# Expert steps of 256 rows with the first-layer weights as the stationary operand, in a mixture-of-experts layer on one Trainium2 core

## The chip, the core and the metric

The kernel runs on one core of one Trainium2 chip. The metric is the device time of one execution in microseconds (us). A core has five engines with instruction streams of their own: TensorE (PE, with its weight loads shown apart as PEld), VectorE (DVE), ScalarE (ACT), GpSimd (POOL) and SyncE (SP, which here only issues transfers). They meet through semaphores. Sixteen DMA engines move the data.

## What is computed

The reference is one transformer layer: attention, a layer norm, a mixture of experts, and a second layer norm. B is 4, L is 2048, D is 256, so there are 8192 tokens.

```python
x = _layernorm(x + attention(x, ...), axis=-1)   # linear (cosformer) attention, 16 heads
# the second part, tokens = x.reshape(-1, 256)
logits = tokens @ router_w.T                     # 8 experts
topv, topi = jax.lax.top_k(logits, 2)
w = jax.nn.softmax(topv, axis=-1)
gate = zeros((T, 8)).at[arange(T)[:, None], topi].add(w)
for e in range(8):
    h = gelu(tokens @ w1[e].T)                   # w1[e] is 512 x 256, exact gelu
    y = h @ w2[e].T                              # w2[e] is 256 x 512
    out = out + gate[:, e:e + 1] * y
x = _layernorm(x + out, axis=-1)
```

## The kernel before

Every product is made in three passes: each operand is split into a high part (a copy to the fp32r type) and a low part (the rest), and high x high, high x low and low x high are summed in PSUM.

**Stage 1** (up to about 302 us) takes the tokens in 32 pairs of 128-row tiles: keys, values, queries, the running attention state, and for pairs nine places back the attention, the output projection, the layer norm and the routing. Each routed token row is scattered (L1602, an indirect DMA of GpSimd) into `expert_rows` in DRAM, in the region of each of its two experts. ScalarE splits one half of the weights of the last expert, GpSimd the rest.

**Stage 2** runs through 135 steps (STEPS) of 128 rows. A table in `steps` says for each step which rows and which expert it takes. For a step s:

- SP's `gather(s)` (L457) loads 128 rows from `expert_rows` into one of NXG = 8 buffers `xg`. First it waits in `freed(s)` until the rows of step s - 8 have been sent, then it reads the row number from the table.
- TensorE turns them (`rows_transposed`, L714, 2 transposes). ScalarE copies the result as the high part of `xgT` (L961), VectorE makes the low part (L1399).
- TensorE makes the hidden layer (`hidden`, L725): the rows are stationary, the weights move in 6 products of 512 columns. ScalarE makes the gelu (L989) into `hg`.
- TensorE turns the gelu (`hidden_transposed`, L755, 4 transposes), ScalarE and VectorE split it into `hT` (L993, L1471).
- TensorE makes the output (`outputs`, L737): 12 products of 256 columns. VectorE multiplies by the gate and adds the row (`gated`, L1407), in place in `xg`. GpSimd sends the rows to `token_rows` by an indirect DMA (`send`, L1683).

TensorE's order is written by hand: turn the rows of s + 1, hidden layer of s, output of s - 1, turn the gelu of s. Between these stand the pieces of the last pairs (attend L578, attention_transposed L601, project_out L630, rank L642 to L646), at places that `hook(s)` gives: from step 7 on six steps for each of eight pairs. VectorE's order in a step is `rows_low(s + 1)`, `gated(s - 1)`, the low part of `hT`, and then the pair's piece. 73 steps (FULL_STEPS) are sure to be full tiles of the first 20 pairs. For the rest a second table is made: `place` on VectorE (L1292 to L1328), a product that turns it (`table_turned`, L697), and a copy (L1332). SP then writes eight tiles of padding rows behind the regions (L484) before it gathers on.

From step 92 on the second layer norm runs beside the experts, in ticks, four to three steps: SP's `load(c)` (L495) fetches 1 MB of `token_rows` for 512 tokens, VectorE sums, takes statistics and scales (L1424, L1430, L1435, L1440), ScalarE normalises (L973) and issues the store (L980). After the last step the remaining chunks follow. The loads are issued by SP too, between its gathers: three at once after gather 96, and then one every three steps.

```python
def freed(s):
    sp.wait_ge(s_y[s % NXG], s // NXG * 16)
```

Of the kernel before, what the change touches and what calls it, by code (L numbers as in the profile page):

```python
# [23 lines left out]
F32 = mybir.dt.float32  # L24
# [9 lines left out]
P = 128  # L34
# [22 lines left out]
REGION = T + P  # L57
STEPS = TOPK * T // P + E - 1
EARLY_PAIRS = NPAIR - PB - 4
FULL_STEPS = 73  # L60
# [5 lines left out]
LEVEL_STEPS = tuple((TOPK * PAIR * n + E * (P - 1)) // P for n in LEVEL_PAIRS)  # L66
TAIL_STEP = LEVEL_STEPS[0] + 5
TICK_STEPS = 3
# [6 lines left out]
for _name, _n in (("ident", P), ("block", P), ("heads", HH), ("experts", E), ("region", E), ("sin", NT_B),  # L75
                  ("cos", NT_B), ("dst", 2 * TOPK), ("step", 1), ("before", P),
                  ("region_parts", E), ("pair", NPAIR),
                  ("upto", E * E)):
    CO[_name] = (NCONST, NCONST + _n)
    NCONST += _n  # L80


def shape_constants():
# [7 lines left out]
    put("block", p[:, None] // HD == p[None, :] // HD)  # L91
# [11 lines left out]
    put("region_parts", np.where(p[:, None] < P - 1, REGION // P - 1, REGION // P + P - 1) * np.arange(E)[None, :])  # L103
# [5 lines left out]
def build(nc, x, xT, WqT, bq, WkT, bk, WvT, bv, WoT, Wo, bo, bo_columns, rwT, w1T, w2T, consts, out):  # L109
    ctx = ExitStack()  # L110
    first = ExitStack()
    ex = nc.dram_tensor("expert_rows", (E * REGION + P, ROW), F32).ap()
    yd = nc.dram_tensor("token_rows", (TOPK * T, D), F32).ap()
    with ctx:
# [11 lines left out]
        gX, gH, gT, gY = bK, bST, bV, bQ  # L126
# [3 lines left out]
        half_neg = sb("half_neg", [4])  # L130
        e_square = sb("e_square", [2])
        gelu_first = sb("gelu_first", [2])
# [4 lines left out]
        tail = sb("tail", [ROW])  # L137
# [17 lines left out]
        steps = sb("steps", [2 * P], I32)  # L155
# [8 lines left out]
        WE = 2 * KD * F  # L164
        HALF = KD * F
        LATE = 1
        EARLY = E - LATE
        NXG = 8
        XG_SLOTS = (2, 3, 4, 0, 1, 5, 6, 7)
        FFN_WORDS = NXG * ROW + 2 * 2 * KD * P + F + 2 * KF * P + 2 * D  # L170
        raws = ExitStack()
        rwk, rwv, rwq, rwo = (sb(n, [KD, D], F32, raws) for n in ("raw_wk", "raw_wv", "raw_wq", "raw_wo"))
        raws.close()
        whole = ExitStack()
        w = sb("w", [E, 2, WE], F32R, whole)
        whole.close()
        sb("w_early_place", [EARLY - 1, 2, WE], F32, first)
        sb("w_high_place", [WE], F32, first)
        wraw = sb("wraw", [2, HALF], F32, first)
# [6 lines left out]
        sb("xraw_begin", [HALF - 3 * D - E - 2 * KD * E], F32, first)  # L186
# [3 lines left out]
        vs = sb("vs", [2, KD, 2, NQ, VQ], F32, first)  # L190
        wk = sb("wk", [2, KD, KE], F32R, first)
        bvb = sb("bvb", [D], F32, first)
        st32 = sb("st32", [KD, 2, NW], F32, first)
# [21 lines left out]
        vare = sb("vare", [2], F32, first)  # L215
        rstd = sb("rstd", [2], F32, first)
# [7 lines left out]
        shift1 = sb("shift1", [2], F32, first)  # L224
        oh = sb("oh", [2, TOPK, E], F32, first)
        dl = sb("dl", [2], F32, first)
        dls = sb("dls", [2], F32, first)
        el = sb("el", [2], F32, first)
        el1 = sb("el1", [2], F32, first)
        idx = sb("idx", [2, 2, TOPK], U32, first)  # L230
        upto_first = sb("upto_first", [1, E, E], F32, first)
# [3 lines left out]
        late = ExitStack()  # L235
        sb("w_place", [EARLY, 2, WE], F32, late)
        w_late_raw = sb("w_late_raw", [LATE, 2, WE], F32, late)
        late.close()
        sb("w_whole_place", [E, 2, WE], F32)
        xgT = sb("xgT", [2, 2, KD, P], F32R)  # L240
        hg = sb("hg", [F])
        sb("xg_place", [2 * D])
        hT = sb("hT", [2, KF, P], F32R)
        sb("xg_begin", [2 * 2 * KD * (NQ - 1)])
        xg = sb("xg", [NXG, ROW])
# [20 lines left out]
        s_wraw = [sem("s_wraw0"), sem("s_wraw1")]  # L266
# [132 lines left out]
        def _(sp):  # L399
# [59 lines left out]
            def freed(s):  # L459

                sp.wait_ge(s_y[s % NXG], s // NXG * 16)

# [1315 lines left out]
```

## Time and profile before

| what | value |
|---|---|
| time, median of 3 runs | 849.87 us (847.88 to 852.35) |
| span of the profiled execution | 841.6 us |
| TensorE busy | 793.9 us, 94% |
| VectorE busy | 566.7 us, 67% |
| ScalarE busy | 461.0 us, 55% |
| GpSimd busy | 434.3 us, 52% |
| DMA | 106.64 MB, 127 GB/s in the mean |
| mean granted TensorE clock | 0.984 of full speed |

The profile shows one execution. Its span is the time from the first to the last instruction and is 8.3 us under the median of the timed runs, which also holds what lies around it. Matmuls are pipelined: the time of a group of n products is n times the pace plus the latency of the last one. Busy times of engines that are not the bound cost nothing in themselves.

### The profile page before, as it was taken

How to read it: one execution, taken by the hardware profiler on the slowest of the kernel's cores; microseconds unless marked ns; L12 is line 12 of the kernel's file. 1: busy time of each engine (PE TensorE's matmuls, PEld its weight loads, DVE VectorE, ACT ScalarE, POOL GpSimd, SP SyncE). 2: the span in 40 equal slices, each digit the busy share in tenths (PEclk: the TensorE clock that was granted, in tenths of full speed). 3: DMA queues.
4: the chain of work that ended last, by engine and by line, in shares of the span. 5: the costliest groups of instructions: out<-in, count | busy, mean ns of one | idle time of the engine just before them, and what ended most of it. 6: DMA issues, size and time to landing. Idle time of an engine off the chain costs nothing.

```text
span 841.6 us, 22076 instructions
## 1 busy us (share of the span) xinstructions
PE 793.9 (94%) x6684; PEld 732.7 (87%) x6684; DVE 566.7 (67%) x1816; ACT 461.0 (55%) x1044; POOL 434.3 (52%) x545
## 2 busy tenths in 40 slices
PE   4999999999999979999999999999999999999990
PEld 4887899899899969999999999989999999999980
DVE  3435788888888857766676666664444477777773
ACT  4656677667777644454444445434444446556663
POOL 3985477677677755544444454542222234444442
PEclk9999999999999989999999999999999999999995
DMA  6444033333333333323323323233322545666644
GB/s 205 160 150 127 26 102 122 113 110 108 108 103 102 98 131 117 119 90 96 99 93 96 108 88 105 87 100 107 99 78 74 179 133 193 228 226 223 220 175 173
DMA packets 56468, 106.64 MB, mean 127 GB/s; under 512 B 9261, under 2 KB 37551, under 8 KB 54448
## 3 DMA queue, kind: packets, MB, share of 16 engines
q1 hardware_dynamic: 41296, 63.25, 24.5%
q0 software_dynamic: 12624, 33.84, 11.0%
q10 hardware_dynamic: 2448, 8.26, 2.7%
q8 instruction: 58, 0.95, 0.5%
q14 instruction: 42, 0.34, 0.1%
HBM read 61.91 MB, written 44.32 MB: 126 GB/s over the span
## 4 chain that ended last, share of the span: by engine, by line
PE 61%; DMA 1%; DVE 1%; ACT 1%; issue 1%; SPq 0%; POOLq 0%; POOL 0%; ACTq 0%
PE PS L737 23%; PE PS L725 22%; PE PS L755 7%; PE PS L714 4%; PE PS L578 2%; PE PS L630 2%; DMA z<-token_rows 1%; PE PS L601 0%; PE PS L541 0%; DMA token_rows<-xg 0%; DMA expert_rows<-rows,idx 0%; PE PS L632 0%; DMA xg<-expert_rows 0%; ACT rows L862 0%; PE PS L614 0%
## 5 line engine op out<-in xcount | busy, mean ns | idle before, releaser
L1683 POOL DMA_INDIRECT token_rows<-xg x135 | 135.1, 1000 | 271.6 <-DVE xg L1407 251.1
L737 PEld LDWEIGHTS PS<-w,hT 128*128 128x128 f32 x1620 | 211.5, 190 | 12.0 <-issue 1.9
L725 PE MATMUL PS<-w,xgT 128*128 x810 | 222.0, 409 | 0.0
L737 PE MATMUL PS<-w,hT 128*128 x1620 | 217.2, 284 | 0.8 <-ACT hT L993 0.8
L725 PEld LDWEIGHTS PS<-w,xgT 128*128 128x128 f32 x810 | 143.2, 189 | 24.6
L1602 POOL DMA_INDIRECT expert_rows<-rows,idx x128 | 133.9, 1046 | 56.1 <-issue 27.8
L993 ACT ACTIVATE hT<-PS 128x512 fp32r<-128x512 f32 x135 | 80.8, 598 | 135.6 <-PE PS L755 135.6
L989 ACT ACTIVATE hg<-PS 128x512 f32<-128x512 f32 x135 | 80.7, 598 | 120.6 <-PE PS L725 120.3
L1471 DVE TENSOR_TENSOR hT<-PS,hT 128x512 fp32r<-128x512 f32 x135 | 93.4, 692 | 75.9 <-ACT hT L993 75.9
L1399 DVE TENSOR_TENSOR xgT<-PS,xgT 128x256 fp32r<-128x256 f32 x135 | 56.9, 422 | 77.8 <-ACT xgT L961 76.3
L755 PE MATMUL PS<-cst,hg 128*128 128x128 f32 x540 | 81.1, 273 | 0.0
L541 PE MATMUL PS<-wk,xs 128*128 128x264 f32 x384 | 64.3, 304 | 14.5 <-DVE wv L1340 8.4
L1407 DVE SCALAR_TENSOR_TENSOR xg<-PS,xg 128x256 f32<-128x256 f32 x135 | 65.0, 482 | 14.0 <-PE PS L737 4.9
L541 PEld LDWEIGHTS PS<-wk,xs 128*128 128x128 f32 x384 | 51.2, 192 | 21.2 <-ACT vs L853 11.8
L578 PE MATMUL PS<-sts,qs 128*128 128x272 f32 x384 | 60.7, 294 | 2.7 <-DVE sts L1091 2.4
L755 PEld LDWEIGHTS PS<-cst,hg 128*128 128x128 f32 x540 | 62.7, 141 | 0.1
L714 PE MATMUL PS<-cst,xg 128*128 128x128 f32 x270 | 52.3, 276 | 5.0 <-DMA xg<-expert_rows 4.0
L541 PE MATMUL PS<-wv,xs 128*128 128x256 f32 x384 | 56.9, 285 | 0.0
L614 PE MATMUL PS<-xs,wq 128*128 128x256 f32 x384 | 56.8, 294 | 0.0
L630 PE MATMUL PS<-wo,aT 128*128 128x264 f32 x384 | 56.5, 286 | 0.0
L578 PEld LDWEIGHTS PS<-sts,qs 128*128 128x128 f32 x384 | 52.0, 191 | 4.0 <-issue 3.0
L961 ACT ACTIVATE xgT<-PS 128x256 fp32r<-128x256 f32 x135 | 51.2, 379 | 3.4 <-PE PS L714 3.4
(179 smaller groups left out, 1272.8 us busy)
## 6 DMA issues: line engine op xcount, KB each, us to landing
xg<-expert_rows SPq DMA_DIRECT2D x135, 130.0 KB, 2.1
z<-token_rows SPq DMA_DIRECT2D x15, 1024.0 KB, 7.8
xraw<-in_xT SPq DMA_DIRECT2D x32, 256.0 KB
xtok<-in_x SPq DMA_DIRECT2D x32, 256.0 KB, 2.8
out_y<-z ACTq DMA_DIRECT2D x15, 512.0 KB, 3.4
wraw<-in_w1T SPq DMA_DIRECT2D x7, 512.0 KB, 3.9
wraw<-in_w2T SPq DMA_DIRECT2D x7, 512.0 KB, 4.0
token_rows<-xg POOLq DMA_INDIRECT x135, 2.6
```

Source lines behind the costliest of these rows:

```text
L541: return nc.tensor.matmul(PS[:, bank, 0:columns], xs[:, rep % 2, a, k, h * P:(h + 1) * P], weights[:, b, k, :], start=(n == 0), stop=(n == ...
L578: mm = nc.tensor.matmul(PS[:, bN + half, 0:2 * NW], qs[:, a, half, h * P:(h + 1) * P], sts[:, b, half].rearrange("p a b -> p (a b)"), star ...
L630: nc.tensor.matmul(PS[:, bank, 0:KE], aT[:, a, k, h * P:(h + 1) * P], wo[:, b, k, :], start=(n == 0), stop=False)
L714: mm = nc.tensor.transpose(PS[:, gX, k * P:(k + 1) * P], xg[:, XG_SLOTS[s % NXG], k * P:(k + 1) * P], ident)
L725: mm = nc.tensor.matmul(PS[:, gH, :], xgT[:, s % 2, a, k, :], w[:, bass.ds(e, 1), b, k * F:(k + 1) * F].rearrange("p o f -> p (o f)"), sta ...
L737: return nc.tensor.matmul(PS[:, gY, 0:D], hT[:, a, k, :], w[:, bass.ds(e, 1), b, HALF + k * D:HALF + (k + 1) * D] .rearrange("p o f -> p ( ...
L755: mm = nc.tensor.transpose(PS[:, gT, k * P:(k + 1) * P], hg[:, k * P:(k + 1) * P], ident)
L989: nc.scalar.activation(hg[:], PS[:, gH, :], ACT.Gelu, scale=2.0).then_inc(gelu_ready, 1)
L993: nc.scalar.activation(hT[:, 0].rearrange("p k t -> p (k t)"), PS[:, gT, :], ACT.Copy)\
L1471: nc.vector.tensor_tensor(hT[:, 1].rearrange("p k t -> p (k t)"), PS[:, gT, :], hT[:, 0].rearrange("p k t -> p (k t)").bitcast(F32), ALU.s ...
L1602: nc.gpsimd.indirect_dma_start(ex, bass.IndirectOffsetOnAxis(ap=idx[:, slot, h, k:k + 1], axis=0), rows[:, slot, h, k, :], None).then_inc( ...
L1683: nc.gpsimd.indirect_dma_start(yd, bass.IndirectOffsetOnAxis(ap=xg[:, XG_SLOTS[s % NXG], C_DST:C_GATE].bitcast(U32), axis=0), xg[:, XG_SLO ...
```

## The change

A step takes 256 rows (TILE), and there are 71 of them. What it does:

- **Hidden layer.** The weights of the first layer are now stationary and the rows move: 24 products of 256 columns for 256 rows, in place of 12 of 512 columns. The result has the hidden units on the partitions, which is the form that the output product wants, so the 8 transposes of the gelu for 256 rows go, and `hidden_transposed` with them.
- **Weights.** The first-layer weights of all experts lie unsplit in `w1`. A step ahead ScalarE (`first_weights_high`) copies the 128x1024 weights of the step's expert as the high part, and VectorE (`first_weights_low`) makes the low part, in two buffers `w1s`. The second-layer weights are split by GpSimd in stage 1, as before, and lie in `w2`. The late split of the last expert at the end of stage 1 goes.
- **Elementwise work.** The gelu and its split stay in two halves of 128x512 each for 256 rows. The split now reads `hg` from SBUF and not from PSUM.
- **Row buffers.** NXG = 4 buffers of 256 rows in place of 8 of 128. A gather moves 256 rows, two neighbouring rows to a partition. Each step's rows go out in two sends, and `gather(s)` waits for both sends of step s - 4.
- **Orders.** TensorE's order in a step is: hidden s (two parts), turn the rows of s + 1 (4 transposes), output of s - 1 (two parts). The pieces of pairs and ticks keep their places in half steps v = 2s and 2s + 1. VectorE's order is `first_weights_low(s + 1)`, `rows_low(s + 1)`, two `hidden_low`, pair part 2s, two `gated(s - 1)`, pair part 2s + 1.
- **Tables.** FULL_STEPS is 33. The eight padding tiles are now 256 rows each, copied from DRAM to DRAM. The first three loads of the second layer norm follow gather 51.
- The mask `block` goes (the constant `heads` is read in its place), and some small tiles share one allocation.

The core of the diff:

```diff
-STEPS = TOPK * T // P + E - 1
+TILE = 2 * P
+REGION = T + TILE
+STEPS = TOPK * T // TILE + E - 1
-FULL_STEPS = 73
+FULL_STEPS = -(-(TOPK * PAIR * EARLY_PAIRS - E * (TILE - 1)) // TILE)
-TAIL_STEP = LEVEL_STEPS[0] + 5
-TICK_STEPS = 3
+TAIL_HALF = 2 * LEVEL_STEPS[0] + 6
+TICK_HALVES = 3
-        NXG = 8
+        NXG = 4
...
-            def gather(s, place):
+            def gather(s):
-                sp.dma_start(xg[:, XG_SLOTS[s % NXG]], ex[bass.ds(row, P), :]).then_inc(s_xg[s % NXG], 16)
+                sp.dma_start(xg[:, XG_SLOTS[s % NXG]], ex[bass.ds(row, TILE), :].rearrange("(p h) c -> p h c", h=2))\
+                    .then_inc(s_xg[s % NXG], 16)
...
-                sp.wait_ge(s_y[s % NXG], s // NXG * 16)
+                sp.wait_ge(s_y[s % NXG], s // NXG * 32)
...
-                sp.dma_start(ex[bass.ds(row, P), :], tail[:]).then_inc(s_tail, 16)
+                sp.dma_start(ex[bass.ds(row, TILE), :].rearrange("(p h) c -> p (h c)", h=2),
+                             ex[E * REGION:, :].rearrange("(p h) c -> p (h c)", h=2)).then_inc(s_tail, 16)
...
-                if s == LEVEL_STEPS[0] + NXG + 1:
+                if s == LEVEL_STEPS[0] + NXG:
                     sent(LEVEL_STEPS[0])
                     for n in range(LOADS):
                         load(n)
                 for c in range(LOADS, LEVEL_CH[1]):
-                    if s == LEVEL_STEPS[0] + NXG + TICK_STEPS * c:
+                    if s == LEVEL_STEPS[0] + NXG + 3 + (TICK_HALVES * (c - LOADS) + 1) // 2:
...
+            def hidden(s, part):
+                if part == 0:
+                    pe.wait_ge(xglo_ready, s + 1)
+                    pe.wait_ge(w1_low, s + 1)
                 if s >= 1:
+                    pe.wait_ge(gelu_ready, 2 * (s - 1) + part + 1)
+                for f in range(2):
+                    c0 = (2 * part + f) * P
+                    m = 0
+                    for k in range(KD):
+                        for a, b in ((0, 0), (1, 0), (0, 1)):
+                            mm = nc.tensor.matmul(PS[:, gH[part], f * TILE:(f + 1) * TILE],
+                                                  w1s[:, s % 2, b, k * F + c0:k * F + c0 + P],
+                                                  xgT[:, s % 2, a, k, :], start=(m == 0), stop=(m == 3 * KD - 1))
...
+            for s in range(STEPS):
+                hidden(s, 0)
+                ranks(2 * s)
+                hidden(s, 1)
+                if s < STEPS - 1:
+                    rows_transposed(s + 1)
+                after = expert(s + 1) if s < STEPS - 1 else None
+                pair_part(2 * s)
+                if s > 0:
+                    outputs(s - 1, before, 0)
+                ranks(2 * s + 1)
+                if s > 0:
+                    outputs(s - 1, before, 1)
+                pair_part(2 * s + 1)
...
+            def first_weights_high(s):
+                if s >= 2:
+                    act.wait_ge(h_done, 2 * (s - 2) + 2)
+                e = nc.values_load(steps[0:1, s:s + 1], engines=[ENG.Activation], min_val=0, max_val=E - 1)
+                nc.scalar.activation(w1s[:, s % 2, 0], w1[:, bass.ds(e, 1)].rearrange("p o f -> p (o f)"), ACT.Copy)\
+                    .then_inc(w1_high, 1)
...
+            def first_weights_low(s):
+                e = nc.values_load(steps[0:1, s:s + 1], engines=[ENG.DVE], min_val=0, max_val=E - 1)
+                dve.wait_ge(w1_high, s + 1)
+                nc.vector.tensor_tensor(w1s[:, s % 2, 1], w1[:, bass.ds(e, 1)].rearrange("p o f -> p (o f)"),
+                                        w1s[:, s % 2, 0].bitcast(F32), ALU.subtract).then_inc(w1_low, 1)
...
-            for s in range(STEPS):
+            for s in range(2 * STEPS):
-                send(s)
+                if s >= 2:
+                    send((s - 2) // 2, s % 2)
```

## Rows read from the trace of the kernel before

**Rows 1.** The page: busy time, share of the span and instructions of each engine.

```profile
PE 793.9 (94%) x6684; PEld 732.7 (87%) x6684; DVE 566.7 (67%) x1816; ACT 461.0 (55%) x1044; POOL 434.3 (52%) x545
```

**Rows 2.** Stretches: length, busy time of each engine, granted clock, DMA share, GB/s.

```profile
350.00:550.00 200.00, 200.00 (x1462) 185.56 (x1461) 135.67 (x419) 96.08 (x191) 99.93 (x124) 1.00 0.31 98
700.00:800.00 100.00, 100.00 (x683) 91.93 (x682) 74.97 (x213) 60.65 (x125) 42.43 (x49) 1.00 0.65 218
```

**Rows 3.** Timeline, one plain step on TensorE: start, duration, engine, line.

```profile
604.20 0.60 PE L755 MATMUL PS<-cst,hg 128*128 128x128 f32 x4
...
604.64 0.38 PE L714 MATMUL PS<-cst,xg 128*128 128x128 f32 x2
...
604.78 1.64 PE L725 MATMUL PS<-w,xgT 128*128 x6
...
606.25 1.60 PE L737 MATMUL PS<-w,hT 128*128 x12
...
607.69 0.60 PE L755 MATMUL PS<-cst,hg 128*128 128x128 f32 x4
```

**Rows 4.** Timeline of ScalarE: the same piece of two pairs, six steps apart.

```profile
374.65 0.59 ACT L871 ACTIVATE aT<-PS 128x512 fp32r<-128x512 f32 x1
...
399.45 0.59 ACT L871 ACTIVATE aT<-PS 128x512 fp32r<-128x512 f32 x1
```

**Rows 5.** Groups by line: VectorE's elementwise work (busy, mean ns, idle before).

```profile
L1471 DVE TENSOR_TENSOR hT<-PS,hT 128x512 fp32r<-128x512 f32 x135 | 93.4, 692 | 75.9 <-ACT hT L993 75.9
L1407 DVE SCALAR_TENSOR_TENSOR xg<-PS,xg 128x256 f32<-128x256 f32 x135 | 65.0, 482 | 14.0 <-PE PS L737 4.9
L1399 DVE TENSOR_TENSOR xgT<-PS,xgT 128x256 fp32r<-128x256 f32 x135 | 56.9, 422 | 77.8 <-ACT xgT L961 76.3
```

**Rows 6.** Timeline where stage 1 ends: the split of 128x1024 weights.

```profile
300.33 1.07 ACT L955 ACTIVATE w<-w_late_raw 128x1024 fp32r<-128x1024 f32 x1
...
301.57 1.78 DVE L1393 TENSOR_TENSOR w<-w_late_raw,w 128x1024 fp32r<-128x1024 f32 x1
...
302.35 3.63 POOL L1613 TENSOR_TENSOR w<-w_late_raw,w 128x256 fp32r<-128x256 f32 x4
...
305.95 0.66 PE L714 MATMUL PS<-cst,xg 128*128 128x128 f32 x2 [3.97 <-DMA xg<-expert_rows]
```

**Rows 7.** Timelines of VectorE, GpSimd and SP: gated, its send, the gather that follows.

```profile
639.33 0.48 DVE L1407 SCALAR_TENSOR_TENSOR xg<-PS,xg 128x256 f32<-128x256 f32 x1
...
640.63 0.97 POOL L1683 DMA_INDIRECT token_rows<-xg  x1 [2.49 <-DVE xg L1407]
...
643.79 0.34 SPq L457 DMA_DIRECT2D xg<-expert_rows  x1
```

**Rows 8.** Transfers, 360 to 500 us: count, KB each, us from issue to landing.

```profile
xg<-expert_rows SPq DMA_DIRECT2D x34, 130.0 KB, 2.1
token_rows<-xg POOLq DMA_INDIRECT x35, 2.5
```

**Rows 9.** Transfers, 700 to 800 us; columns as in rows 8.

```profile
z<-token_rows SPq DMA_DIRECT2D x10, 1024.0 KB, 7.7
token_rows<-xg POOLq DMA_INDIRECT x29, 5.0
```

**Rows 10.** DMA, 671 to 672.5 us: the first three loads under way, a gather behind.

```profile
DMA packets 86, 0.66 MB, mean 437 GB/s; under 512 B 6, under 2 KB 6, under 8 KB 6
...
xg<-expert_rows SPq DMA_DIRECT2D x1, 130.0 KB, 4.7
```

**Rows 11.** Timeline at the second table: `place` on VectorE, and TensorE's wait.

```profile
558.61 0.41 DVE L1292 TENSOR_TENSOR o<-cst,seg_len 128x256 f32<-128x256 f32 x1
...
562.08 0.15 DVE L1328 TENSOR_SCALAR table<-table 128x1 f32<-128x1 f32 x1
...
562.29 0.38 PE L697 MATMUL PS<-cst,table 128*2 128x128 f32 x2 [1.33 <-DVE table L1328]
```

**Rows 12.** Timeline of SP: the eight padding tiles.

```profile
582.05 8.36 SPq L484 DMA_DIRECT2D expert_rows<-tail  x8
```

More of the change, by code:

```diff
@@ L214, in build @@
         mv = sb("mv", [2, 2], F32, first)
-        vare = sb("vare", [2], F32, first)
-        rstd = sb("rstd", [2], F32, first)
+        pairs = sb("pairs", [8, 2], F32, first)
+        vare, rstd, shift1, dl, dls, el, el1 = (pairs[:, n] for n in range(7))
         rows = sb("rows", [2, 2, TOPK, ROW], F32, first)
@@ L815, in _ @@
                         table_turned(SECOND_MADE, bA)
-            outputs(STEPS - 1, before)
+            before, now = None, expert(0)
+            for s in range(STEPS):
[12 more added lines that the diff above has]
+                pair_part(2 * s + 1)
+                before, now = now, after
+            for h in range(2):
+                outputs(STEPS - 1, before, h)
         @block.scalar
@@ L1019, in _ @@
                         normalise(j, j // 2, True, j % 2)
-                for t in ticks(s):
+                for t in ticks(v):
                     tail_part(t)
+            for s in range(STEPS):
+                if s < STEPS - 1:
+                    first_weights_high(s + 1)
+                for part in range(2):
+                    gelu(s, part)
+                if s < STEPS - 1:
+                    rows_high(s + 1)
+                for part in range(2):
+                    hidden_high(s, part)
+                pair_part(2 * s)
+                pair_part(2 * s + 1)
             for t in TICKS_LEFT:
@@ L1321, in place @@
                 made(base + 12)
[L1322 removed]
+                nc.vector.scalar_tensor_tensor(out=table[:, 1:2], in0=const("step"), scalar=float(TILE), in1=table[:, 1:2],
                                                op0=ALU.mult, op1=ALU.add).then_inc(table_step, 1)
@@ L1331, in steps_from @@
                 dve.wait_ge(tbl_done, which + 1)
-                nc.vector.tensor_copy(steps[0:2, which * P:(which + 1) * P], PS[0:2, bank, P:2 * P])\
+                begin, end = ((0, FULL_STEPS), (FULL_STEPS, P))[which]
+                nc.vector.tensor_copy(steps[0:2, begin:end], PS[0:2, bank, P:P + end - begin])\
                     .then_inc(table_step, 1)
@@ L1566, in _ @@
                     tail_part(t)
-            gated(STEPS - 1)
+            for s in range(STEPS):
+                if s < STEPS - 1:
+                    first_weights_low(s + 1)
+                    rows_low(s + 1)
+                for part in range(2):
+                    hidden_low(s, part)
+                pair_part(2 * s)
+                if s > 0:
+                    for h in range(2):
+                        gated(s - 1, h)
+                pair_part(2 * s + 1)
+            for h in range(2):
+                gated(STEPS - 1, h)
             for t in TICKS_LEFT:
@@ L1696, in tail_part @@
                     deviation(c)
-            for s in range(STEPS):
+            for s in range(2 * STEPS):
                 if s < 2:
@@ L1740, in _ @@
                     tail_part(t)
+            for h in range(2):
+                send(STEPS - 1, h)
             for t in TICKS_LEFT:
```

390 lines of the change are left out of this document (172 added, 218 removed).

## The prediction

> **What bounds the kernel now.** I read the page first: TensorE is busy for 94% of the span, the next engine for 67% [rows 1]. Then the stretches: from 350 to 550 us and from 700 to 800 us TensorE has no idle time and the full clock [rows 2]. So stage 2 takes what TensorE's instructions take, and the timeline of one plain step gives their pace [rows 3]. The step is 607.69 - 604.20 = 3.49 us (3.48 below). A group of n products lasts n - 1 paces and one latency, so the 12 products of 256 columns, which start 1.44 us ahead of the next group, have a pace of 0.120 us. The 6 of 512 columns take 1.47 us, the four transposes of the gelu 0.44 us (0.109 each), the two of the rows 0.14 us up to the start of the hidden layer. In the steps with pairs six steps take 399.45 - 374.65 = 24.80 us [rows 4], so that a pair's pieces take 24.80 - 6 x 3.48 = 3.9 us of TensorE.
>
> **TensorE's work after.** 256 rows need 24 + 24 products of 256 columns and 4 transposes: 48 x 0.120 + 4 x 0.109 = 6.20 us, against 6.96 us for two steps before. No row shows these stationary weights with moving rows, but the shape is that of the output product, so I take its pace. The bounds are 0.107 (256 columns at 2.4 GHz) and 0.123 (half of 1.47 / 6) for the hidden layer's 24: 5.9 to 6.3 us. But there are 71 steps for 135 / 2 = 67.5, because each expert's last tile is padded to 256 rows: 71 x 6.20 = 440.2 against 135 x 3.48 = 469.8. That is **-29.6 us**, and it is all that the change can win. (The Trainium skill, "TensorE: Matmul & The Clock Gate", section "Back-to-back issue gap", speaks against the exchange of 12 products of 512 columns for 24 of 256: in a stream of weight loads and products it has 0.131 us for 512 columns and 0.081 for 128, about 0.098 for 256 in between, an estimate from that page. By it the hidden layer goes from 1.57 to 2.35 us for 256 rows, 55 us more in 71 steps, where the rows have 2.94 and 2.88 us, 4 us less; the forecast would be some 925 us. The trace does not agree: it has 0.245 and 0.120 us, nearly in proportion to the columns, and it decides.)
>
> The pipeline holds a step of rows more at each end, and a step is twice as long. The last output takes 2.9 us for 1.4, and a second send follows it; the first gather, transposes and split are larger by some 1 us. **+4 us.** Stage 1 is bound by TensorE too and loses only work of GpSimd, ScalarE and VectorE that lies beside it: 0.
>
> **VectorE.** An operation of 512 columns takes 0.69 us, of 256 0.42 us [rows 5], so one of 1024 about 1.24 us; the one row with 1024 has 1.78 us, with GpSimd at its own split beside it [rows 6]. I take 1.24, as GpSimd's splits are over. A step costs 1.24 + 0.69 (rows) + 0.69 + 0.61 (gelu) + 0.48 + 0.42 (gated) = 4.1 us. A pair's pieces are 135.7 / 200 x 24.80 = 16.8 less 6 x 1.60, 7.2 us [rows 2, 5]. Three steps then hold 12.4 + 7.2 = 19.6 us in 3 x 6.20 + 3.9 = 22.5: it fits, but not evenly. The step with halves 1 and 2 of a pair has over half of the 7.2 us: 4.1 + 3.9 = 8.0 against 6.20 + 1.2 on TensorE, which waits for the attention's result. I take 0.8 us for each of eight pairs, and 0.2 for sends that GpSimd's scatters hold up: **+8 us** (0 to 16). (A rule of the Trainium skill speaks against these splits: "SBUF — State Buffer", section "Who interferes with whom", says that a VectorE instruction with two SBUF inputs and a GpSimd one that reads SBUF block each other. The 1.78 us agree with it. With 1.78 in each step three steps hold 21.2 us, still under 22.5.) ScalarE has 1.07 us of new copy [rows 6] and at most 5.7 us in a step: cover enough.
>
> **The row buffers.** This is where I expect the gain to go. Rows of step s must be out before gather(s + 4). After the output of s TensorE has hidden, transposes, output, hidden before it needs the rows of s + 4: 3 x 2.88 + 0.44 = 9.1 us. Before it had eight steps less two, over 20 us. The chain now: gated 0.5; the first send starts 640.63 - 639.81 = 0.8 later; the second is 1.3 behind it (0.97 and a gap); landing 2.5 [rows 8]; SP issues 643.79 - 640.63 - 2.5 = 0.7 after that [rows 7]; a gather of 130 KB lands in 2.1 [rows 8]. Twice the rows with twice the run for a descriptor I put at 2.5, between 2.1 and 4.2. Sum: 8.3 us. It fits by 0.8 us where nothing disturbs it.
>
> From the second layer norm on something does. The send's median landing goes from 2.5 to 5.0 us while loads of 1 MB are in flight, 7.7 us each [rows 9]. In the new order a load stands right behind a gather, and both sends that free the next buffer fall into it. 2.5 more less 0.8 to spare, and tick work of VectorE ahead of `gated`, up to 0.9: about 2 us for each of the ten loads c = 3 to 12, **+20 us** (5 to 30). The first three loads stand between gathers 51 and 52. 3.15 MB at 437 GB/s are 7.2 us, and a gather behind them took 4.7 us where 2.1 is usual [rows 10, 8]. With four buffers gather 52 is needed 6.2 us after gather 51 was: **+6 us** (3 to 8).
>
> **The second table.** `place` takes 558.61 to 562.23, 3.6 us, and TensorE waits 1.33 us at its end [rows 11], since the turning product comes a step later. After, both stand in one step, and TensorE comes to it as VectorE begins: +2.3 us. Then the eight padding tiles take SP 8.4 us [rows 12], plus 2 for landing and 0.7, between gathers 32 and 33, where 6.2 + 0.8 are to be had, partly under the first stall: +3.2. **+5.5 us** (2 to 10).
>
> **The clock.** After an idle stretch of 4.0 us TensorE's first transposes took 0.66 for 0.38 us [rows 6, 3], which is the 1.2 GHz level. Three of the new stalls are that long. I take **+2 us** (0 to 8).
>
> **Sum.** -29.6 + 4 + 8 + 20 + 6 + 5.5 + 2 = +15.9 us. The profiled 841.6 us become 857.5; with the 8.3 us by which the median stands above its span, 866.
>
> **The rivals.**
> A. *The buffers never run out*: sends land as fast as before or the loads leave room. Then -29.6 + 4 + 7 + 2.3 = -16: 833 to 834 us, faster. For it: the plain steps fit. Against it: the landing of 5.0 us. It decides if the chain stays under 9.1 us with a load in flight. 0.18.
> B. *The loads cost a quarter*: 0.5 us each, 5 in place of 20: 851 us. It would be so if only one of the two sends meets the load. 0.13.
> C. *The gather of 256 rows takes 3.5 to 4.2 us*. The chain is 9.3 to 10.0 us, over 9.1 in every step, shared over the two steps of the loop: up to 0.45 us in 43 steps outside the pairs, 20 us more: 886 us. For it: twice the bytes. Against it: the fixed part is not doubled. 0.12.
> D. *VectorE becomes the bound in the ticks*, in place of the buffers. The 683 products from 700 to 800 us are 28.5 steps and 38 ticks, so a tick costs it (74.97 - 28.5 x 1.60) / 38 = 0.8 us [rows 2, 5]; 2.7 ticks and 4.1 us are 6.2 us a step, level with TensorE, and 6.8 with the slow split: 0 to 13 us in 21 steps upon A, 840 in the middle. 0.09.
>
> The forecast has 0.48, within 856 to 880 us.
>
> **Range and chances.** About 0.5% is what a measurement of this kernel can tell from no change: 845.6 to 854.1. Faster: A, most of D: 0.25. Same: most of B and a little of the forecast's low end and of D: 0.11. Slower: 0.64. Cases of both signs hold most of the chance, so the range reaches into A: 838 to 886.
>
> **What would show it.** Product starts 0.120 us apart in the hidden layer, and plain steps of 6.2 us, confirm TensorE's part. In the windows from the first tick on TensorE should show idle time ended by the DMA of `xg` (some 25 us in all), at L714's successor, and none in the plain steps between table and ticks; sends should land in about 5 us there. If TensorE has no such waits, A holds; waits in plain steps too speak for C; waits of TensorE for VectorE's `xgT` or `w1s` in the ticks for D. At the second table there should be a wait of over 3 us for `table`, and one for `xg` after it. The prediction is wrong above all if a send and a load in flight share the DMA engines otherwise than in the rows.

## The result, and the profile after

The changed kernel takes 943.64 us (932.11 to 948.42), the one before 849.54 in the same runs: **a ratio of 1.102, 95% interval 1.096 to 1.108**. Two of the four runs of the changed kernel, over 1.5% above its fastest, are left out of the ratio, by which the change costs some 86 us; comparisons below go by such ratios, each against the kernel before as it ran beside that variant, times 846 us, about its time throughout. The forecast of 866 us, and the top of its range, 886, are far too low. The profiled execution took 932.1 us, with a span of 930.3.

The page, its busy times and two of its rows of 40 slices, to be held against [rows 1]:

```profile
PE 801.9 (86%) x7136; PEld 761.2 (82%) x7136; DVE 622.1 (67%) x1836; ACT 529.6 (57%) x1064; POOL 454.9 (49%) x517
...
PE   5999999999998688888889888878999978888880
...
PEclk9999999999999799999999999989999999989995
```

TensorE is busy for 86% of a longer span, and it holds 8 us more of busy time than before where the sum said 30 less. Three stretches, with the columns of [rows 2]: pair steps, plain steps, ticks.

```profile
350.00:550.00 200.00, 172.20 (x1369) 166.08 (x1368) 136.93 (x358) 106.42 (x174) 106.93 (x110) 0.97 0.28 87
640.00:700.00 60.00, 56.29 (x442) 53.95 (x441) 32.61 (x51) 32.41 (x53) 21.91 (x18) 0.97 0.26 80
740.00:850.00 110.00, 92.36 (x685) 88.56 (x684) 76.97 (x187) 63.04 (x106) 43.73 (x42) 0.92 0.50 177
```

There is idle time in each, in the plain steps too, where the forecast had none. What ended TensorE's idle time from 306 us on (engine, line, releaser; total us, times, longest):

```profile
PE PS L698 <- DMA xg<-expert_rows: 57.4, 31, 4.5
PE PS L562 <- DVE qs L1211: 6.8, 6, 1.6
PE PS L726 <- issue: 5.4, 23, 0.4
PE PS L626 <- DVE o L1072: 3.9, 1, 3.9
```

31 times the transposes of the rows (L698, in the kernel before L714) wait for a gather. The longest of these waits, 4.5 us for the very first rows, is no loss of the change: the kernel before has it too, with 3.97 us [rows 6]. The other 30 are new. One plain step, followed from its last output product to the step that takes its buffer (timelines of VectorE, GpSimd, SP and TensorE; steps 37 and 41):

```profile
661.37 3.04 PE L713 MATMUL PS<-xgT,w1s 128*128 128x256 f32 x24
...
661.57 0.88 DVE L1448 SCALAR_TENSOR_TENSOR xg<-PS,xg 128x256 f32<-128x256 f32 x2 [0.94 <-PE PS L726]
...
662.88 1.55 POOL L1710 DMA_INDIRECT token_rows<-xg  x1 [4.20 <-DVE xg L1448]
664.73 0.97 POOL L1710 DMA_INDIRECT token_rows<-xg  x1 [0.30 <-issue]
...
667.85 0.33 SPq L437 DMA_DIRECT2D xg<-expert_rows  x1
...
664.25 0.60 PE L698 MATMUL PS<-cst,xg 128*128 128x128 f32 x4
664.61 3.11 PE L726 MATMUL PS<-w,hT 128*128 x24
...
670.78 0.66 PE L698 MATMUL PS<-cst,xg 128*128 128x128 f32 x4 [0.19 <-DMA xg<-expert_rows]
671.64 3.23 PE L726 MATMUL PS<-w,hT 128*128 x24 [0.20 <-issue]
```

The chain is 670.78 - 661.57 = 9.21 us from the start of `gated`, for the predicted 8.3. To it come the 0.20 us for which TensorE is already at its next hidden layer (661.37) before `gated` starts: 9.41. The room, which counts from there, is 9.1. And behind a wait the output products start 0.86 us after the transposes (671.64 - 670.78), without one 0.36 (664.61 - 664.25).

A wait costs more than itself. After 2.54 us the output group takes 3.91 us for 3.11; the granted clock is 0.65 from 434 to 438 us and 0.93 from 438 to 442:

```profile
434.47 0.66 PE L698 MATMUL PS<-cst,xg 128*128 128x128 f32 x4 [2.54 <-DMA xg<-expert_rows]
...
436.61 3.91 PE L726 MATMUL PS<-w,hT 128*128 x24
```

To see where the time lies I read the starts of the low split of the rows (L1431) off VectorE's timeline in each run's profiled execution, and took differences between steps (us, us a step in brackets). Steps 3 to 30 hold the pairs, 30 to 39 the second table and what follows it, 50 to 52 the first three loads, 52 to 70 the ticks. Each row is a single execution, and two of them can differ by several us in a stage that the edit does not touch: `small_loads` has 81.0 us from step 39 to 50 and the changed kernel 73.6. Differences of that size between rows show nothing by themselves.

```
                            3-30          30-39        39-50        50-52       52-70
changed kernel (4 buffers)  251.0 (9.30)  75.0 (8.3)   73.6 (6.69)  17.4 (8.7)  143.7 (7.98)
sends_together              231.8 (8.59)  72.8 (8.1)   73.3 (6.66)  17.9 (9.0)  140.7 (7.82)
sends_together_ticks        234.8 (8.70)  70.4 (7.8)   73.6 (6.69)  18.9 (9.5)  136.3 (7.57)
expert_read_early           250.7 (9.29)  69.1 (7.7)   74.6 (6.78)  15.8 (7.9)  140.1 (7.78)
no_weight_low               244.4 (9.05)  68.5 (7.6)   76.0 (6.91)  17.0 (8.5)  135.1 (7.51)
small_loads                 251.2 (9.30)  74.5 (8.3)   81.0 (7.36)  16.7 (8.4)  139.8 (7.77)
four_mended                 221.6 (8.21)  69.8 (7.8)   77.6 (7.05)  16.7 (8.4)  136.3 (7.57)
four_all_mends              210.2 (7.79)  67.9 (7.5)   73.1 (6.65)  17.6 (8.8)  129.6 (7.20)
five_buffers                233.3 (8.64)  65.0 (7.2)   68.1 (6.19)  12.4 (6.2)  117.8 (6.54)
six_buffers                 231.7 (8.58)  62.6 (7.0)   68.1 (6.19)  12.4 (6.2)  111.4 (6.19)
six, second half early      207.4 (7.68)  60.6 (6.7)   68.1 (6.19)  12.4 (6.2)  111.4 (6.19)
```

### The profile page after: what moved, and what is told of

Same layout as the page of the kernel before. It is cut to its first block, busy times and chain, and to the rows that moved or that the text cites. A ratio compares the mean times of both kernels' runs of the same rounds, so it can differ in the third digit from the quotient of the medians.

```text
span 930.3 us, 21892 instructions
## 1 busy us (share of the span) xinstructions
PE 801.9 (86%) x7136; PEld 761.2 (82%) x7136; DVE 622.1 (67%) x1836; ACT 529.6 (57%) x1064; POOL 454.9 (49%) x517
## 4 chain that ended last, share of the span: by engine, by line
DMA 14%; PE 14%; issue 14%; DVE 6%; POOL 4%; SPq 3%; ACT 1%; POOLq 0%; DVEq 0%; ACTq 0%
PE PS L726 9%; DMA token_rows<-xg 8%; DMA xg<-expert_rows 6%; PE PS L713 3%; POOL token_rows L1710 2%; PE PS L698 2%; DVE xg L1448 2%; SPq L436 2%; DVE hT L1439 1%; DVE xgT L1431 1%; SPq L437 1%; DMA z<-token_rows 1%; POOL zve L1716 1%; POOL expert_rows L1646 1%; DVE z L1465 1%
## 5 line engine op out<-in xcount | busy, mean ns | idle before, releaser
L713 PE MATMUL PS<-xgT,w1s 128*128 128x256 f32 x1704 | 220.6, 286 | 1.8 <-DVE xgT L1431 1.8
L713 PEld LDWEIGHTS PS<-xgT,w1s 128*128 128x128 f32 x1704 | 212.6, 194 | 2.6 <-DVE xgT L1431 2.4
L1431 DVE TENSOR_TENSOR xgT<-PS,xgT 128x512 fp32r<-128x512 f32 x71 | 49.0, 691 | 139.8 <-ACT xgT L965 116.4
L1423 DVE TENSOR_TENSOR w1s<-w,w1s 128x1024 fp32r<-128x1024 f32 x71 | 86.9, 1224 | 22.2 <-issue 16.1
L698 PE MATMUL PS<-cst,xg 128*128 128x128 f32 x284 | 47.3, 292 | 57.5 <-DMA xg<-expert_rows 57.4
L1439 DVE TENSOR_TENSOR hT<-hg,hT 128x512 fp32r<-128x512 f32 x142 | 91.2, 684 | 1.7 <-issue 1.7
L698 PEld LDWEIGHTS PS<-cst,xg 128*128 128x128 f32 x284 | 33.1, 147 | 64.5 <-DMA xg<-expert_rows 59.8
L978 ACT ACTIVATE hT<-hg 128x512 fp32r<-128x512 f32 x142 | 81.4, 626 | 0.0
L965 ACT ACTIVATE xgT<-PS 128x512 fp32r<-128x512 f32 x71 | 42.3, 596 | 65.8 <-PE PS L698 60.7
L956 ACT ACTIVATE w1s<-w 128x1024 fp32r x71 | 74.9, 1055 | 6.9 <-issue 5.5
L853 ACT ACTIVATE rows<-xtok,pairs 128x512 f32<-128x512 f32 x64 | 48.9, 820 | 17.8 <-POOL pairs L1669 17.1
```

The costliest lines, as they stand in the source:

```text
L698: mm = nc.tensor.transpose(PS[:, gX, k * TILE + h * P:k * TILE + (h + 1) * P], xg[:, XG_SLOTS[s % NXG], h, k * P:(k + 1) * P], ident)
L713: mm = nc.tensor.matmul(PS[:, gH[part], f * TILE:(f + 1) * TILE], w1s[:, s % 2, b, k * F + c0:k * F + c0 + P], xgT[:, s % 2, a, k, :], sta ...
L978: nc.scalar.activation(hT[:, s % 2, 0, 2 * part:2 * part + 2].rearrange("p k t -> p (k t)"), hg[:, 2 * part:2 * part + 2].rearrange("p k t ...
L1423: nc.vector.tensor_tensor(w1s[:, s % 2, 1], w1[:, bass.ds(e, 1)].rearrange("p o f -> p (o f)"), w1s[:, s % 2, 0].bitcast(F32), ALU.subtrac ...
L1439: nc.vector.tensor_tensor(hT[:, s % 2, 1, 2 * part:2 * part + 2].rearrange("p k t -> p (k t)"), hg[:, 2 * part:2 * part + 2].rearrange("p ...
```

## The experiments

**Six buffers.** The theory was that too few row buffers cost the most; the rival was that the time would come back as waits for VectorE.

```diff
-        NXG = 4
-        XG_SLOTS = (2, 3, 1, 0)
+        NXG = 6
+        XG_SLOTS = (4, 5, 3, 2, 1, 0)
```

> The changed kernel with six row buffers of 256 rows (XG_SLOTS = (4, 5, 3, 2, 1, 0)) in place of four; nothing else changes. In its trace TensorE waits 57 us for the DMA of xg, has some 23 us of other new idle time, and its products cost some 38 us more than at the full clock. Theory 'too few buffers': with two more steps of room (9.1 us become over 21) the waits for xg go, and with them most of the time at the lower clock: 845 to 870 us, granted clock near 1. Rival 'VectorE and GpSimd are late anyway': the waits for xg turn into waits for VectorE's xgT, qs and o, and for the table: 895 to 925 us. Rival 'the sends themselves are too slow for any number of buffers': waits for xg stay above 30 us, 925 to 943 us.

857.71 us, ratio 1.014 (1.011 to 1.018): 74 us less. (The first loads now follow gather 53 and no longer 51, since their place counts from NXG, but they wait for the same sends.) In its windows and on its page:

```profile
350.00:550.00 200.00, 177.75 (x1500) 174.34 (x1499) 149.52 (x397) 112.81 (x186) 113.07 (x116) 1.00 0.30 93
600.00:660.00 60.00, 60.00 (x506) 60.00 (x505) 37.61 (x59) 36.07 (x59) 23.98 (x20) 1.00 0.29 90
700.00:800.00 100.00, 100.00 (x842) 100.00 (x841) 92.98 (x229) 76.56 (x133) 56.29 (x52) 1.00 0.71 238
...
PE 769.0 (90%) x7136; PEld 742.2 (87%) x7136; DVE 619.7 (73%) x1836; ACT 524.8 (61%) x1064; POOL 460.6 (54%) x517
```

From 600 to 800 us TensorE stands idle no more, with the loads in flight, and each step takes 6.19 us: the predicted 6.20. The busy time falls from 801.9 to 769.0 us for the same 7136 products. So of the 75.8 us between the spans 33 are no idle time at all, but the same products taking longer; the mean granted clock goes from 0.958 to 0.978. VectorE, busy for 93 of 100 us in the ticks, is no bound there: rival D falls.

**Five buffers.**

> The changed kernel with five row buffers (XG_SLOTS = (3, 4, 2, 1, 0)). From gated of step s to the transposes of the step that takes its buffer the trace of the changed kernel has 13.0 us on the mean in the pair steps, 9.9 in the plain ones and 11.6 in the ticks. With four buffers TensorE has 9.1 us of other work in that time, with five 15.3, with six 21.5. Theory 'the chain against the room': the mean chains fit into 15.3, so five do as well as six: 855 to 865 us. Rival 'it is the longest chains and not the means': 870 to 890 us.

863.82 us, 1.019 (1.016 to 1.022): within the first theory. The ticks are longer than with six (6.54 for 6.19 us a step): there two waits for `xg` are left, so single long chains count and not only the mean one.

**What makes the chain long.** GpSimd works in order, and between the two sends of a pair step stand the half deviation or scatters (timeline of GpSimd, changed kernel):

```profile
451.40 1.04 POOL L1710 DMA_INDIRECT token_rows<-xg  x1 [4.20 <-DVE xg L1448]
452.51 0.19 POOL L1664 TENSOR_SCALAR pairs<-mv 128x2 f32<-128x2 f32 x1
452.78 0.22 POOL L1665 TENSOR_SCALAR pairs<-mv 128x2 f32<-128x2 f32 x1
453.09 1.54 POOL L1667 TENSOR_TENSOR pairs<-pairs,exponents 128x2 f32<-128x2 f32 x1
454.71 0.59 POOL L1669 TENSOR_TENSOR pairs<-pairs 128x2 f32<-128x2 f32 x1
455.47 1.32 POOL L1710 DMA_INDIRECT token_rows<-xg  x1 [0.17 <-issue]
```

The second send starts 4.07 us after the first. I moved everything that stands between them behind the second, and then the ticks' deviations too:

```diff
                 if s >= 2:
                     send((s - 2) // 2, s % 2)
...
-                if j is not None:
-                    if n == 3:
-                        half_deviation(j)
...
+                if s % 2 == 1:
+                    other_work(s - 1, *hook(s - 1))
+                    other_work(s, *hook(s))
```

> The changed kernel with GpSimd's two sends of a step one right behind the other; the scatters and the half deviation that stand between them come after the second. In the pair steps the second send starts 2.6 to 4.3 us after the first, in the plain ones 1.85. Theory 'GpSimd's order holds up the second send': 1 to 2 us less in the chain of the 20 or so steps where other work stands between, 918 to 930 us, and the waits for xg before 550 us at half. Rival 'the landing, not the start, is late': within 5 us of 943. Rival 'what is put off is late next' (the layer norm's scale for ScalarE, the scatters): slower than 948.

918.54 us, 1.088 (1.085 to 1.091): 12 us less by the ratios, 24 between the profiled spans. The pair steps fall from 9.30 to 8.59 us, which is what six buffers give, and their waits for `xg` from 21.3 to 1.5 us: in these steps GpSimd's order was about the whole of the buffers' loss. Over the whole run the waits for `xg` fall from 57.4 to 31.4 us.

> The kernel sends_together (918.5 us), and the layer norm's deviation, which stands between the two sends in every third tick step, comes after both too. In the ticks the second send starts 3.4 us after the first in those steps and 1.3 in the others. Theory 'GpSimd's order, not the loads, makes the ticks slow': the ticks, 18 steps in 141 us, fall by 0.5 us each or more: 903 to 912 us. Rival 'it is VectorE's tick work or the traffic of loads and outputs': 915 to 921 us.

912.32 us, 1.079 (1.076 to 1.083), 7 us less again, and the edit touches the ticks alone. GpSimd's order is a small part of their 32 us.

**The loads**, on which 20 us of the forecast rested. The later loads move a quarter of the bytes; the sums of the other rows are made of old data.

```diff
+                if LOADS <= c < LAST_CH:
+                    sp.dma_start(z2[:, c % LOADS, 0:1], y_chunks[c, :, 0:1]).then_inc(s_z[c % LOADS], 16)
+                elif c < LAST_CH:
-                if c < LAST_CH:
                     sp.dma_start(z2[:, c % LOADS], y_chunks[c]).then_inc(s_z[c % LOADS], 16)
```

> The changed kernel with the second layer norm's loads 3 to 14 a quarter of the size (256 KB, the sums of the other rows are made of old data); VectorE's work stays. The tick steps take 8.1 us on the mean, the plain ones 6.65. Theory 'loads delay the sends': the ticks fall to 6.7 us, 21 x 1.4 = 29 us less: 910 to 920 us. Rival 'VectorE's tick work delays gated and the splits': within 5 us of 943.

930.55 us, 1.098 (1.093 to 1.103): not to be told from 1.102, and between the two expectations, 910 to 920 us and within 5 us of 943. The ticks take 139.8 us for 143.7, which is within what single executions differ by; by the two intervals the size of the loads is worth some 10 us at most, of the ticks' 32. From the start of the second send to that of the gather it takes 4.1 us on the mean of steps 52 to 65 in the changed kernel, for 3.4 in its plain steps 33 to 45; here it is 3.8 for 3.7. So sends do land later with the full loads in flight, by 0.7 us in the mean. SyncE itself is not busy elsewhere: of its waits in the ticks all but 0.8 us are for the sends.

**VectorE's weight split beside the send.** The first send of the plain step above takes 1.55 us; in [rows 7] it is 0.97. Beside it VectorE subtracts the weights (L1423; step 36, timelines of VectorE and GpSimd):

```profile
655.34 1.22 DVE L1423 TENSOR_TENSOR w1s<-w,w1s 128x1024 fp32r<-128x1024 f32 x1
...
655.85 1.55 POOL L1710 DMA_INDIRECT token_rows<-xg  x1 [3.36 <-DVE xg L1448]
```

In this run it does so for steps 0 and 1 in full and later for 8 columns, so that old low parts are multiplied from step 2 on.

```diff
-                nc.vector.tensor_tensor(w1s[:, s % 2, 1], w1[:, bass.ds(e, 1)].rearrange("p o f -> p (o f)"),
-                                        w1s[:, s % 2, 0].bitcast(F32), ALU.subtract).then_inc(w1_low, 1)
+                n = slice(0, HALF if s < 2 else 8)
+                nc.vector.tensor_tensor(w1s[:, s % 2, 1, n], w1[:, bass.ds(e, 1), n].rearrange("p o f -> p (o f)"),
+                                        w1s[:, s % 2, 0, n].bitcast(F32), ALU.subtract).then_inc(w1_low, 1)
```

> The changed kernel, in which VectorE subtracts the low part of the first-layer weights only for steps 0 and 1, and later for 8 of 1024 columns: the low weights of an old step are multiplied, so that the time alone is told by it. It takes 1.2 us of VectorE from each step and an instruction with two SBUF inputs from beside the first send, which takes 1.55 us there where 0.97 was usual. Theory 'port': the first send falls to about 1.0 us and the chain is 0.6 us shorter in each step: 920 to 935 us. Theory 'VectorE is late': 1.2 us less in each of the 25 pair steps and of the tick steps: 895 to 915 us, and the waits for qs, o and xgT go. If neither is at work: 938 to 945.

916.93 us, 1.084 (1.080 to 1.087): 15 us less. GpSimd's timeline, and the row of VectorE beside it:

```profile
658.73 0.97 POOL L1711 DMA_INDIRECT token_rows<-xg  x1 [3.93 <-DVE xg L1449]
660.01 0.98 POOL L1711 DMA_INDIRECT token_rows<-xg  x1 [0.31 <-issue]
...
658.22 0.16 DVE L1424 TENSOR_TENSOR w1s<-w,w1s 128x8 fp32r<-128x8 f32 x1
```

The send is back at 0.97 and the second stands 1.28 behind it, for 1.85: the subtraction, with both inputs in SBUF, had held up the send by 0.58 us. (The Trainium skill, "SBUF — State Buffer", section "Who interferes with whom": a VectorE instruction with two SBUF inputs contends with a GpSimd one that reads SBUF. The 0.58 us agree with that rule; the forecast cited it and priced it for VectorE alone.) The run takes 1.2 us of work from VectorE in each step as well. Whether that helps too isn't shown: in the pair steps the waits for `qs` fall from 6.8 to 3.0 us, but those for `o` rise from 1.2 to 6.0, and what falls in all is the wait for `xg`, from 21.3 to 14.6.

**TensorE's read of the expert's number** stands between transposes and output products, in order.

```diff
                 hidden(s, 1)
+                if s + 1 == FULL_STEPS:
+                    pe.wait_ge(table_step, SECOND_TABLE)
+                after = expert(s + 1) if s < STEPS - 1 else None
                 if s < STEPS - 1:
                     rows_transposed(s + 1)
-                after = expert(s + 1) if s < STEPS - 1 else None
```

> The changed kernel with four buffers; TensorE reads the expert's number of step s + 1 ahead of the transposes of s + 1 and no longer behind them. In the trace the output's products start 0.36 us after the transposes where TensorE has not waited, and 0.86 where it has waited for xg, however short. Theory 'the read of the table is in the open after every wait, and lengthens the cycle of the buffers': 0.5 us less behind each of some 45 waits, 918 to 930 us. Rival 'those 0.5 us are the refilling of TensorE's own pipeline or something else': 939 to 947 us.

924.64 us, 1.094 (1.090 to 1.097). By the ratios that is 7 us, by the profiled spans 10: about half of the 14 to 26 that the expectation takes off 943.6, though the median lies in its range. Its mechanism shows: behind a wait the products now start 0.41 us after the transposes.

```profile
684.12 0.66 PE L698 MATMUL PS<-cst,xg 128*128 128x128 f32 x4 [0.99 <-DMA xg<-expert_rows]
684.53 3.12 PE L726 MATMUL PS<-w,hT 128*128 x24
```

**The two mends on four buffers.**

> Four buffers; both sends of a step together with all of GpSimd's other work behind them, and the expert's number read ahead of the transposes: the two mends that were tried alone. Alone they gave 31 us (912.3) and 19 us (924.6) against 943.6. If the two are parts of one cycle that simply add: 943.6 - 31 - 19 = 893, 888 to 900 us. If one takes away the waits on which the other depends (fewer waits, so fewer reads in the open): 900 to 910. If the shorter cycle falls under TensorE's own work in most steps, as with five buffers: under 880.

891.56 us, 1.056 (1.051 to 1.062): 38 us less by the ratios, where the two alone gave 19 and 7 by the same measure. They do more than add, mostly in the pair steps (8.21 us); by the intervals the surplus is 13 us, give or take 8.

**VectorE's order in the pair steps**, on six buffers. What TensorE waits for there, from 350 to 550 us:

```profile
PE PS L585 <- DVE o L1083: 10.6, 7, 1.8
PE PS L562 <- DVE qs L1211: 9.8, 7, 1.9
```

That is 2.9 us for each of seven pairs, where the forecast had 0.8. The first attempt moved `query_low` ahead of the splits and the attention's sine and cosine parts ahead of the hidden layer's splits, and mended the table, the rank and the read of the expert's number:

```diff
+                if j is not None and n == 5 and j < NPAIR - 1:
+                    query_low(j + 1, j + 1 - GROUP_PAIRS)
                 if s < STEPS - 1:
                     first_weights_low(s + 1)
                     rows_low(s + 1)
+                if hook(2 * s)[1] == 1:
+                    pair_part(2 * s)
                 for part in range(2):
                     hidden_low(s, part)
```

> Six buffers, and in the second stage: query_low ahead of the splits in its step; the sine part and the attention's normalisation (VectorE) and the cosine part (ScalarE) ahead of hidden_low and hidden_high; the second table's place a half step earlier; the first rank a half step later; the expert's number read ahead of the transposes. In the run with six buffers TensorE waits 9.8 us for qs, 11.1 and 3.9 for o, 5.1 for the table. Theory 'only VectorE's order stands between that run and the predicted 6.2 us a step': most of the 30 us go, 828 to 838 us, faster than the kernel before. Rival 'VectorE has too much to do in the pair steps': the waits move to xgT and w1s: 845 to 858 us.

856.42 us, 1.011 (1.008 to 1.014): the rival's time, but not its mechanism. The waits for `qs` are gone, and it is not `xgT` and `w1s` that TensorE waits for instead; those for `o` have doubled:

```profile
PE PS L585 <- DVE o L1089: 20.4, 7, 3.9
```

The next run leaves the move of the sine and cosine parts out.

> The kernel six_buffers_reordered without its move of the attention's sine and cosine parts: six buffers, query_low ahead of the splits, the second table's place earlier, the first rank later, the expert's number read early. Theory 'the move did the harm' (in its trace ScalarE stands idle up to 2.2 us ahead of the cosine part, and TensorE waits 20.9 us for o in place of 11.1): the gains at the table, the rank and qs stay, 840 to 848 us. Rival 'whatever TensorE does not wait for at qs it waits for at o, as the pair's chain sets the pace': 852 to 858.

836.67 us, 0.992 (0.990 to 0.994), below the range of the theory: that move alone had cost 16 us, and the others give 19. Why the move harms is open. In its trace ScalarE's cosine part, free to start by the other engines' records, stands idle behind something that the trace doesn't resolve:

```profile
425.20 0.49 ACT L826 ACTIVATE tcos<-PS,cst 128x272 f32<-128x272 f32 x1 [1.54 <-remote]
```

What does help is to give the chain from the attention's products to its transposes more time: the second half's products (n = 1) stand between the two parts of the hidden layer. (The diff shows TensorE's part first, then ScalarE's, then VectorE's; the layer norm's scaling on ScalarE moves a step later to make place.)

```diff
             def ranks(v):
...
+                if j is not None and n == 1:
+                    attend(j, LAG + j, 1)
...
                 gelu(s, 0)
+                if j is not None and n == 1:
+                    cos_part(j, LAG + j, 1)
                 gelu(s, 1)
                 if s < STEPS - 1:
                     rows_high(s + 1)
+                if n == 1 and 2 * s > FIRST_GROUP + 1:
+                    done = NPAIR - 1 if j is None else j - 1
+                    normalise(done, done // 2, True, done % 2)
...
                 first_weights_low(s + 1)
+                if j is not None and n == 1:
+                    add_sin_part(j, LAG + j, 1)
+                    normalise_attention(j, LAG + j)
                 rows_low(s + 1)
```

> As the kernel before it in this list, and the second half of the attention's products (n = 1) between the two parts of the hidden layer, the cosine part right behind the first gelu, the sine part and the normalisation ahead of rows_low, and the layer norm's scaling (normalise) a step later, behind rows_high. TensorE now gets the second half 3 us earlier, so that o is ready before its transposes. Theory 'the chain from the products to the transposes sets the pair steps': the waits for o and qs go, three pair steps take 23.4 us in place of 25.7, 9 times: 822 to 832 us. Rival 'ScalarE or VectorE is full in those steps': the waits move to xgT and w1s, 845 to 858 us.

**828.73 us, 0.982 (0.980 to 0.984): faster than both kernels.** The waits for `o` and `qs` between 350 and 550 us are gone; the pair steps take 7.68 us for 7.50 of TensorE's own work:

```profile
350.00:550.00 200.00, 195.71 (x1671) 194.59 (x1670) 165.71 (x456) 125.01 (x206) 131.16 (x132) 0.99 0.36 109
600.00:700.00 100.00, 100.00 (x842) 100.00 (x841) 70.21 (x127) 60.33 (x100) 43.17 (x36) 1.00 0.40 128
```

**All of it on four buffers**, and SP reads the place of a gather before it waits for the buffer: is the number of buffers the cause, or the length of the chain?

```diff
+                row = place_of(s)
                 freed(s)
-                gather(s)
+                gather(s, row)
```

> Four row buffers as in the changed kernel, with all that shortens or unloads the chain: sends together with GpSimd's other work behind, TensorE's read of the expert's number ahead of the transposes, the order of VectorE and ScalarE of six_buffers_second_half_early, and new: SP reads the place of a gather before it waits for the buffer (its read and checks stand 0.7 us ahead of each gather, behind that wait). In a plain step the chain from the last output product to the transposes was 0.3 + 1.3 + 1.85 + 3.0 + 2.8 = 9.25 us against 9.1 us of room; now 8.55. Theory 'a tenth of a microsecond decides: a chain under 9.1 fits': plain steps of 6.2 us, ticks and pair steps near it (their chains fall to about 8.6 too, but for scatters): 840 to 855 us. Rival 'single long landings and not the usual chain decide, and each is followed by time at the lower clock': plain steps of 6.5 and more, 865 to 885 us.

864.62 us, 1.027 (1.023 to 1.030): the rival, at its lower end. Most plain steps are now free of waits, as a chain under 9.1 would have it, but three of the eleven from 39 to 50 are not (TensorE's timeline):

```profile
658.80 0.61 PE L702 MATMUL PS<-cst,xg 128*128 128x128 f32 x4
659.16 3.12 PE L730 MATMUL PS<-w,hT 128*128 x24
...
666.72 0.66 PE L702 MATMUL PS<-cst,xg 128*128 128x128 f32 x4 [1.56 <-DMA xg<-expert_rows]
667.13 3.11 PE L730 MATMUL PS<-w,hT 128*128 x24
```

From the start of the second send to that of SP's gather there are 2.57 to 2.62 us after ten of the fourteen steps 33 to 46, 3.3 after one, and 4.5 to 4.7 after three: sends that land 2 us late, with no load in flight. Five and six buffers hide them: there the plain steps have no wait at all. What delays them was not tried. So both are causes: the long chain, mended here for 64 us by the ratios, and the room, which six buffers give on top (38 us more in the same order).

## Why the prediction was wrong

By the ratios the change costs 86 us where the sum said 16. Of these 70 us the buffers make 43 (74 measured, 31 in the sum), and the other 27 stand with six buffers too; the new order of the pair steps and the table wins back 27.

- **TensorE's products (-29.6 us): right.** 6.19 us a step against 6.20 in three stages, once nothing else holds it.
- **The ends (+4): about right.** From the last output product to the end there are 23.7 us for 20.6.
- **The row buffers (9.1 us of room, 8.3 of chain, "fits by 0.8"): the step that failed.** They cost 74 us; the sum has 20 + 6 for the loads, 3.2 at the table and 0.2 a pair, some 31. Piece by piece in a plain step: `gated` and first send 1.31 (predicted 1.3); second send 1.85 behind (1.3), as the weight split holds up the first; landing and SP 3.1 (3.2); gather to transposes 2.9 (2.5); and 0.2 us from TensorE's next hidden layer to `gated` that I left out. Three errors of 0.2 to 0.6 us, all one way, turned 0.8 to spare into 0.3 missing, so that even plain steps wait. That is the sign that I had named for rival C, but the gather is only a third of it.
- **"0.2 for sends that GpSimd's scatters hold up": far too small.** On the mean the second send starts 3.3 us after the first in the pair steps, which is 2 us more in the chain. Put together, the sends give 19 us there between the profiled executions, all that six buffers give.
- **The later loads (+20): wrong cause.** The ticks lose 32 us to the buffers, but the loads' size has at most some 10 of them. The step in it that failed is the send's landing, put at 2.5 us later with a load in flight: the gathers follow the second send 0.7 us later than in the plain steps (4.1 for 3.4, means). Besides, in every third step the layer norm's deviation stands between the sends, and the second starts 3.4 us after the first, for 1.3 to 1.4 in the others. How the 32 us divide between GpSimd's order (some 7), the late landings and VectorE's tick work is open.
- **The first three loads (+6):** 17.4 - 12.4 = 5.0 us. Right.
- **The pair steps (+8): the second step that failed.** 48.5 us over 27 x 7.50, of which 19.3 go with two more buffers and 24.3 with the order of VectorE, ScalarE and TensorE. I had compared VectorE's work with TensorE's over three steps and added 0.8 us a pair; what counts is the chain from the second half's products by way of ScalarE and VectorE to the transposes, with 3 us of cover.
- **The second table (+5.5):** from step 30 to 39 the changed kernel takes 12.4 us more than with six buffers, where the sum has 3.2 for the buffers, and 14.4 more than with the place earlier as well. Too small again; the buffers' part for the same reason.
- **The clock (+2): far too small.** The granted clock's mean is 0.958 against 0.978 with six buffers; over their spans that is (0.042 x 930.3 - 0.022 x 854.5) x 2 = 41 us more at the 1.2 GHz level. I had counted three long waits; there are 30 new ones. Work at half the clock takes twice its time, so the 41 us explain at most half their length, some 20 of the 33 us of longer busy time. The rest comes with the waits at the full clock too: from 658.75 to 732.3 us (steps 39 to 50) the granted clock is 1.00, and TensorE is busy for 71.4 us for the 68.1 that eleven steps take with six buffers. That this is the restart behind each wait is likely, but not shown. Together the 33 us are almost as much as the 43 us of idle time that they came with.
- Rival B had the loads cheap, and they are; the time is lost at the other stations of the same chain. Rival A (the buffers never run out) is tested by six buffers, and they take 858 us and not 833, since the pair steps were mis-sized as well. That the mended orders on six buffers come to 829 and 837 us, around A's number, is partly luck: they hold moves that A did not have.

## What to carry to other kernels

Halving the number of buffers while doubling what each holds keeps the bytes and cuts the room: count, from the last reader to the next user, every engine that the buffer passes with what stands in its queue, and want some microseconds to spare rather than 0.8, since single landings come 2 us late. Where the bound engine's slack is gone, a wait costs more than its length, as its products take longer after it: here 43 us of idle time came with 33 us of longer busy time. Reads of tables into registers belong ahead of the wait, not behind it.

## What the runs showed of the hardware

- A send of 128 rows by GpSimd takes 0.97 us, and 1.55 where VectorE's subtraction with two SBUF inputs of 1024 columns stands beside it.
- A register read of TensorE that stands behind a wait costs 0.45 us before the next products (0.86 against 0.41), and nothing where TensorE has work queued.
- Products of 256 columns keep a pace of 0.120 us with new weights for each, whether the weights of the layer or its rows are stationary: 48 of them and 4 transposes take 6.19 us with six buffers.
- With 30 more waits for rows, of 0.2 to 4.1 us, the mean granted clock was 0.958 for 0.978. After one wait of 2.54 us it was 0.65 in the mean from 434 to 438 us.
- Three of fourteen sends of 128 rows landed some 2 us later than the rest, with no load in flight.
